# Second mixture normalises and transposes its finished tiles itself; the normalisation stage behind it is dropped

## The chip, the cores and the metric

The kernel runs on one core of a Trainium2 chip, as one program. The metric is the device time of an execution in microseconds (us). Three runs of the kernel before gave 3135.24, 3126.11 and 3123.97, median 3126.11.

## The reference, cut to what matters

Four gated layers run over x, 32 tiles of 128 rows by 128 features (float32); each layer is a cross attention and a mixture, and each adds its output to x. The change lies between the mixture of layer 1 (the second mixture) and the attention of layer 2:

```python
x = x + tanh(g_ffn[1]) * L1_ffn(layernorm(x))          # the mixture
lat = layer_norm(layernorm(x), ln_l_g, ln_l_b)          # input of layer 2's attention
q = lat @ Wq;  k, v = split(concat([ctx_normed, lat], axis=1) @ Wkv)

def L1_ffn(x):      # 8 experts, the two best of each row, and a shared one
    for e in range(8):   # each expert: 64 hidden columns
        y = (silu(x @ gate[e].T) * (x @ up[e].T)) @ down[e].T
        out += where(row chose e, y * mean_weight[e], 0)
    return out + mlp(x, shared weights)                  # 128 hidden columns
```

The attention's own input is thus x normalised twice, scaled by ln_l_g and shifted by ln_l_b. Two normalisations in a row are done as one, with the power -0.5 of var * (1 + eps) + eps * eps.

## The kernel before, in words

x (`k.x`) stays in SBUF, 32 tiles. The program is a sequence of stages; each is a block with one instruction stream for each engine, the engines meet at its end, and nothing of the next stage starts earlier. At the start of a stage SyncE's stream clears the semaphores of the stage before it (`zero_last_stage`, line 93), one instruction each, and only then issues its loads. Inside a stage each engine takes its instructions strictly in the written order and waits on semaphores.

`l1_mixture` (line 1613) is the second mixture. It reads the transposed, normalised input from `k.cols`, and works in 8 groups of four tiles (512 columns, one PSUM bank). For each group it has 5 units: c = 0 to 3 are pairs of experts, c = 4 is the shared one.

- TensorE, `layers` (1673): a gate product and an up product of 128 x 512 for each unit, into two banks used in turn, so unit n waits until `silu_done` and `multiplied` of unit n-2. Behind it, for units 0 to 3 of all groups but the last, `keys.project` (137) computes keys of a later stage. After unit 1 of group g it runs `output(g-1)` (1682), 20 products down to the four tiles, into bank `y_ps[g % 2]`. `output(7)` is the last.
- ScalarE: the silu of each gate product (1713), then, for the units that have one, the copy of the projected keys (151), which waits until the DMA of the slot's last keys has landed.
- GpSimd: for units 0 to 3 the product of the gate with the 0/1 mask of the experts (1659). After unit 3 of each group a product that scales weights of a later stage (1664).
- VectorE: gate times up (1743), and after unit 2 of group g `add(g-1)` (1725): x of group g-1 plus the gated output from PSUM (1728), and four `bn_stats` (1732).
- SyncE: stores the keys (156) and loads masks (1640), in turn. A load waits for the mask product that frees its slot.

Then comes `l2_cross` (3043). It calls `normalise_measured` (433) with twice=True, a stage of its own ("n2a" in the names of tiles): VectorE works means and variances out of the `bn_stats` of all 32 tiles (473 to 482), GpSimd takes the power -0.5, eight tiles at a time (line 571 in the profile), VectorE and ScalarE normalise tiles into staging buffers (496, 544), TensorE transposes four tiles into a bank (513), ScalarE copies the bank to `k.cols` with gain and shift (558). `l2_attention` (1750) follows; its first products read `k.cols` (1895, 1903), and its scores (1868) wait for keys loaded by DMA (1828).

## Time and profile before

| | |
|---|---|
| median of three runs | 3126.11 us (3123.97 to 3135.24) |
| profiled execution, first to last instruction (span) | 3116.6 us |
| busy: TensorE 91%, weight loads 72%, VectorE 65%, ScalarE 58%, GpSimd 46% | of the span |
| second mixture, first gate product to last addition | 956.9 to 1096.5 us |
| stage between mixture and attention | 1096.9 to 1110.7 us |
| first product of the attention | 1110.94 us |

The profile gives the span of one execution, taken by the hardware profiler, and for this execution no time of its own beside the span; the runs are timed from outside, so that their median lies 9.5 us above the span. An engine is busy while one of its instructions runs; waits are listed as idle time, with the instruction that ended them. "PE" is TensorE, "PEld" its weight load, "DVE" VectorE, "ACT" ScalarE, "POOL" GpSimd, "SPq" a DMA issued from SyncE. A float32 matmul is recorded as two. PEclk is the granted TensorE clock as a share of 2.4 GHz.

### The profile page before, as it was taken

The page shows a single profiled execution, that of the slowest core. Times are in us where ns is not written, and L with a number is a line of the kernel's source. Part 1 is how long each engine was busy: PE and PEld are TensorE (multiplying, and loading weights), DVE is VectorE, ACT ScalarE, POOL GpSimd, SP SyncE. Part 2 cuts the span into 40 slices and gives each one's busy share as a digit, 9 for nine tenths or more (in the row PEclk, how much of TensorE's full clock was granted, in tenths as well). Part 3 has the DMA queues.
Part 4 walks back from the last instruction along what each step waited for, and adds up shares of the span by engine and source line. Part 5 has one row for each costly group of instructions (what it writes and reads, how often), then busy time and mean ns, then how long its engine had stood idle before and what let it go on. Part 6 is the DMA issues. An engine that isn't in the chain of part 4 may idle for free. (4 is left out here: it accounts for less than half of the span.)

```text
span 3116.6 us, 70141 instructions
## 1 busy us (share of the span) xinstructions
PE 2851.3 (91%) x21784; PEld 2258.1 (72%) x21784; DVE 2019.9 (65%) x7949; ACT 1821.4 (58%) x5322; POOL 1426.3 (46%) x1719
## 2 busy tenths in 40 slices
PE   7999969977998989999999899999999996597999
PEld 5888854434775678888888777888888774486676
DVE  4554436664653356666666469999999999486433
ACT  5777734443553256666666467887888873353333
POOL 2122217762542334444444247878787876552000
PEclk9999979987998999999999898989999985597999
DMA  3000023433763311111111000000000000001000
GB/s 114 6 5 6 5 68 70 81 81 118 264 224 101 118 49 54 56 54 55 56 54 50 13 14 10 14 14 14 13 13 14 14 14 32 2 19 36 7 10 10
DMA packets 99484, 152.01 MB, mean 49 GB/s; under 512 B 11312, under 2 KB 39488, under 8 KB 98752
## 3 DMA queue, kind: packets, MB, share of 16 engines
q1 hardware_dynamic: 99296, 149.96, 16.0%
q8 instruction: 62, 1.02, 0.1%
q14 instruction: 126, 1.03, 0.1%
HBM read 103.33 MB, written 46.47 MB: 48 GB/s over the span
## 5 line engine op out<-in xcount | busy, mean ns | idle before, releaser
L1845 POOL TENSOR_TENSOR l2a_probs<-l2a_probs,l2a_inv 128x1024 f32<-128x1024 f32 x128 | 242.3, 1893 | 371.7 <-DVE l2a_inv L2011 371.7
L1956 ACT ACTIVATE l2a_probs<-l2a_s_ps,l2a_nm 128x256 f32<-128x256 f32 x512 | 236.1, 472 | 199.4 <-DVE l2a_nm L1987 199.3
L2700 DVE MAX8 l3a_top<-l3a_work 128x8 f32<-128x128 f32 x1536 | 314.6, 279 | 0.0
L2486 PEld LDWEIGHTS l3a_l2o_ps<-net_arena 128*128 128x128 f32 x2016 | 275.3, 222 | 51.2 <-issue 40.3
L2355 POOL TENSOR_SCALAR l3a_above<-l3a_score,l3a_top 128x128 f32<-128x128 f32 x512 | 298.8, 601 | 16.4 <-DVE l3a_work L2702 6.5
L2486 PE MATMUL l3a_l2o_ps<-net_arena 128*128 128x128 f32 x2016 | 283.5, 308 | 15.8 <-ACT net_l1f_gate L2562 15.8
L2702 DVE MATCH_REPLACE8 l3a_work<-l3a_top,l3a_work 128x128 f32<-128x128 f32 x1024 | 269.2, 277 | 0.0
L2474 PE MATMUL l3a_l2h_ps<-net_cols,net_arena 128*128 (+1 forms) x1024 | 251.0, 388 | 12.0 <-ACT net_arena L2593 10.5
L2474 PEld LDWEIGHTS l3a_l2h_ps<-net_cols,net_arena 128*128 128x128 f32 x1024 | 185.0, 191 | 64.8 <-ACT net_arena L2593 23.5
L721 ACT ACTIVATE l0a_probs<-l0a_score_ps,l0a_nm 128x128 f32<-128x128 f32 x512 | 179.6, 381 | 75.1 <-DVE l0a_nm L770 75.1
L2593 ACT ACTIVATE net_arena<-l3a_l2h_ps,net_l2f_b 128x256 f32<-128x256 f32 x512 | 210.0, 492 | 16.6 <-PE l3a_l2h_ps L2474 13.7
L2467 PEld LDWEIGHTS l3a_o_ps<-l3a_v,l3a_pT 128*128 128x128 f32 x1024 | 149.7, 218 | 75.7 <-ACT l3a_pT L2552 66.2
L755 POOL TENSOR_TENSOR l0a_v<-l0a_v,l0a_inv 128x1024 f32<-128x1024 f32 x32 | 60.8, 1901 | 301.2 <-DVE l0a_inv L794 301.2
L2467 PE MATMUL l3a_o_ps<-l3a_v,l3a_pT 128*128 128x9 f32 x1024 | 149.4, 274 | 51.7 <-ACT l3a_pT L2552 51.7
L2360 POOL TENSOR_TENSOR l3a_probs<-l3a_probs,l3a_above 128x512 f32<-128x512 f32 x128 | 162.8, 1272 | 44.1 <-ACT l3a_probs L2571 34.5
L1987 DVE TENSOR_REDUCE l2a_nm<-l2a_s_ps 128x2 f32<-128x512 f32 x256 | 159.0, 683 | 28.4 <-PE l2a_s_ps L1868 28.3
L2571 ACT ACTIVATE l3a_probs<-l3a_score,l3a_nm 128x128 f32<-128x128 f32 x512 | 156.1, 395 | 22.3 <-POOL l3a_nm L2339 22.0
L770 DVE TENSOR_REDUCE l0a_nm<-l0a_score_ps 128x4 f32<-128x512 f32 x128 | 82.2, 684 | 125.5 <-PE l0a_score_ps L681 125.5
L2170 DVE SCALAR_TENSOR_TENSOR net_x<-l3f_o_ps,net_weight,net_x 128x128 f32 (+1 forms) x256 | 72.2, 345 | 139.8 <-PE l3f_o_ps L2087 139.3
L2122 ACT ACTIVATE l3f_hidden<-l3f_h_ps 128x512 f32<-128x512 f32 x128 | 76.3, 597 | 146.0 <-PE l3f_h_ps L2078 146.0
L1919 PE MATMUL l2a_side_ps<-net_ident,l2a_probs 128*128 128x128 f32 x1024 | 153.5, 280 | 1.1 <-POOL l2a_probs L1845 0.7
L2087 PEld LDWEIGHTS l3f_o_ps<-net_arena,l3f_hidden 128*128 128x128 f32 x1024 | 124.2, 192 | 29.7 <-issue 18.2
(527 smaller groups left out, 7184.4 us busy)
## 6 DMA issues: line engine op xcount, KB each, us to landing
kv_ahead<-l1a_kept SPq DMA_DIRECT2D x128, 256.0 KB, 2.6
l0f_code<-code_rows SPq DMA_DIRECT2D x32, 512.0 KB, 10.9
l2a_kT<-kv_ahead SPq DMA_DIRECT2D x64, 256.0 KB, 2.6
l2a_v<-kv_ahead SPq DMA_DIRECT2D x64, 256.0 KB, 2.6
l1a_shift<-neg_top SPq DMA_DIRECT2D x16, 512.0 KB, 4.7
l1f_chosen<-mask_code SPq DMA_DIRECT2D x64, 128.0 KB, 3.1
keys_ahead<-l1f_keys_kept SPq DMA_DIRECT2D x32, 256.0 KB, 3.2
l3a_kT<-keys_ahead SPq DMA_DIRECT2D x32, 256.0 KB, 2.7
```

The source lines that it names most:

```text
L721: act.activation(probs[c % 2][:, h, :], score[g][:, i * P:(i + 1) * P], ACT.Exp, bias=nm[:, h:h + 1], accum_out=sums[c % 2][:, h:h + 1]).t ...
L1845: pool.tensor_tensor(p[:, :, :], p[:, :, :], per_row(inv[c % 2][a][:, :, :].rearrange("p i o -> p (i o)"), KV), ALU.mult).then_inc(scaled, 1)
L1956: act.activation(probs[c % 2][a][:, 2 * i + odd, :], s_ps[a][odd][:, i * KV:(i + 1) * KV], ACT.Exp, bias=nm[c % 2][a][:, i, odd:odd + 1], ...
L1987: dve.tensor_reduce(nm[c % 2][a][:, :, odd:odd + 1].rearrange("p i o -> p (i o)"), s_ps[a][odd][:, :].rearrange("p (i s) -> p i s", i=2), ...
L2355: ins = pool.tensor_scalar(above[:, i, :], score[c % 4][:, h, :], top[c % 2][:, ROUNDS - 1, h, 7:8], None, ALU.is_ge)
L2360: pool.tensor_tensor(probs[c % 2][:, hs, :], probs[c % 2][:, hs, :], above[:, :, :], ALU.mult).then_inc(masked, 1)
L2467: ins = pe.matmul(o_ps[:, h, :], pT[n % 2][:, i, :], v[c % 4][:, h, :], start=True, stop=True)
L2474: ins = pe.matmul(h_ps[i][:, n * WIDE:(n + 1) * WIDE], w1[:, expert(u, x), 2 * i + n, :], k.cols[:, ds(group(q, u) * WIDE, WIDE)], start=T ...
L2486: ins = pe.matmul(output_bank(u, x)[:, at:at + D], hidden[2 * x + n][:, i, j * P:(j + 1) * P], w2[:, expert(u, 2 * x + n), i, :], start=(i ...
L2593: ins = act.activation(hidden[x][:, 2 * i + n, :], h_ps[i][:, n * WIDE:(n + 1) * WIDE], ACT.Gelu, bias=b1[:, e, 2 * i + n:2 * i + n + 1])
L2700: ins = dve.max(t[:, step // 2, h, :], src)
L2702: ins = dve.match_replace(work[:, h, :], t[:, step // 2, h, :], src, LOWEST)
```

## The change

Group g is now normalised and transposed inside the mixture. VectorE's `add` writes its `bn_stats` to a local tile; a new `spread(g)` takes mean and variance with four `bn_aggr` and one `tensor_scalar`; GpSimd's `inverse_std(g)` takes the power -0.5 of four values a row; VectorE's `norm_rows(g)` normalises four tiles; TensorE's `turn(g)` transposes them into the output bank `y_ps[g % 2]`, which is free by then; ScalarE's `take_cols(g)` copies the bank to `k.cols` with gain and shift. `output` waits for that copy in place of the addition. `spread(g-1)` follows unit 3 of group g; `inverse_std(g-1)` follows unit 3's mask, ahead of the weight scaling; `norm_rows(g-2)` follows unit 0, `turn(g-2)` and `take_cols(g-2)` unit 2. Two groups are left for the end. The call of `normalise_measured` goes.

```diff
@@ l1_mixture
+        stats, mean_var, veps, rstd = (s.sb(n, [P, G4, w]) for n, w in (("stats", 6), ("mean_var", 2), ("veps", 1), ("rstd", 1)))
+        normed = s.sb("normed", [P, G4, D])
+        gain, shift = k.l2n_w.norms[:, 2:3], k.l2n_w.norms[:, 3:4]
+        x_measured, moments, veps_ready, rstd_ready, rows_ready, turned, cols_ready = (s.sem(n) for n in (
+            "x_measured", "moments", "veps_ready", "rstd_ready", "rows_ready", "turned", "cols_ready"))
@@ gpsimd
+                def inverse_std(g):
+                    pool.wait_ge(veps_ready, g + 1)
+                    pool.wait_ge(rows_ready, G4 * g)
+                    pool.tensor_tensor(rstd[:, :, 0], veps[:, :, 0], k.neg_half[:, 0:G4], ALU.pow).then_inc(rstd_ready, 1)
...
-                    if g == 0:
+                    if g:
+                        inverse_std(g - 1)
+                    else:
                         pool.wait_ge(scaled, E)
                         wn.wait(pool)
                     pool.tensor_tensor(wn.w2[:, g, :, :], wn.w2[:, g, :, :], per_group(wn.scale_all[:, g, :], 4), ALU.mult
                                        ).then_inc(next_scaled, 1)
                 pool.tensor_tensor(wn.bias8[:, :], wn.bias8[:, :], wn.scale8[:, :], ALU.mult).then_inc(next_scaled, 1)
+                inverse_std(NG - 1)
@@ tensor
-                        pe.wait_ge(y_used, g - 1)
+                        pe.wait_ge(cols_ready, g - 1)
...
+                def turn(g):
+                    pe.wait_ge(rows_ready, G4 * (g + 1))
+                    for j in range(G4):
+                        ins = pe.transpose(y_ps[g % 2][:, j * P:(j + 1) * P], normed[:, j, :], k.ident[:, :])
+                    ins.then_inc(turned, 1)
...
                         layers(g, c)
+                        if c == 2 and g >= 2:
+                            turn(g - 2)
...
+                turn(NG - 2)
                 output(NG - 1)
+                turn(NG - 1)
@@ scalar
+                def take_cols(g):
+                    act.wait_ge(turned, g + 1)
+                    act.activation(k.cols[:, g * BANK:(g + 1) * BANK], y_ps[g % 2][:, :], ACT.Identity, scale=gain, bias=shift
+                                   ).then_inc(cols_ready, 1)
...
+                        if c == 2 and g >= 2:
+                            take_cols(g - 2)
                         if c < PAIRS and g + 1 < NG:
                             keys.take(act, (g + 1) * PAIRS + c)
+                take_cols(NG - 2)
+                take_cols(NG - 1)
@@ vector
-                    for t in range(g * G4, (g + 1) * G4):
-                        dve.bn_stats(k.stats[:, t, :], k.x[:, t, :]).then_inc(k.measured, 1)
+                    for j in range(G4):
+                        dve.bn_stats(stats[:, j, :], k.x[:, g * G4 + j, :]).then_inc(x_measured, 1)
+                def spread(g):
+                    dve.wait_ge(x_measured, G4 * (g + 1))
+                    for j in range(G4):
+                        dve.bn_aggr(mean_var[:, j, :], stats[:, j, :]).then_inc(moments, 1)
+                    dve.wait_ge(moments, G4 * (g + 1))
+                    dve.tensor_scalar(veps[:, :, 0], mean_var[:, :, 1], 1.0 + LN_EPS, LN_EPS * LN_EPS, ALU.mult, ALU.add
+                                      ).then_inc(veps_ready, 1)
+                def norm_rows(g):
+                    dve.wait_ge(rstd_ready, g + 1)
+                    if g:
+                        dve.wait_ge(turned, g)
+                    for j in range(G4):
+                        dve.tensor_scalar(normed[:, j, :], k.x[:, g * G4 + j, :], mean_var[:, j, 0:1], rstd[:, j, :],
+                                          ALU.subtract, ALU.mult).then_inc(rows_ready, 1)
...
                         if c == 2 and g:
                             add(g - 1)
+                        if c == 3 and g:
+                            spread(g - 1)
+                        if c == 0 and g >= 2:
+                            norm_rows(g - 2)
+                norm_rows(NG - 2)
                 add(NG - 1)
+                spread(NG - 1)
+                norm_rows(NG - 1)
@@ l2_cross
-    norms = k.l2n_w.norms
-    normalise_measured(nc, k, "n2a", gains=k.l2n_w, twice=True, gain=norms[:, 2:3], shift=norms[:, 3:4])
     l2_attention(nc, k)
```

## Rows read from the trace of the kernel before

**Rows 1.** Busy time of each engine in three stretches, with granted clock, DMA share, GB/s.
```profile
1050.00:1075.00 25.00, 25.00 (x133) 17.18 (x132) 7.90 (x17) 7.20 (x13) 10.05 (x8) 1.00 0.36 123
1075.00:1096.00 21.00, 18.07 (x100) 12.26 (x98) 6.64 (x14) 3.96 (x7) 6.70 (x6) 1.00 0.16 60
1096.00:1112.00 16.00, 7.17 (x39) 5.42 (x40) 8.97 (x38) 9.14 (x17) 6.53 (x4) 0.77 0.01 2
```
**Rows 2.** Timeline, group 5 into 6: start, duration, instruction, idle time before and its releaser.
```profile
1071.49 0.74 DVE L1728 SCALAR_TENSOR_TENSOR net_x<-l1f_y_ps,net_tg,net_x 128x512 f32<-128x512 f32 x1
1073.49 0.69 DVE L1743 TENSOR_TENSOR l1f_hidden<-l1f_u_ps,l1f_gate 128x512 f32<-128x512 f32 x1 [0.36 <-POOL l1f_gate L1659]
1076.28 0.69 DVE L1743 TENSOR_TENSOR l1f_hidden<-l1f_u_ps,l1f_gate 128x512 f32<-128x512 f32 x1 [2.10 <-ACT l1f_gate L1713]
1076.81 1.27 POOL L1659 TENSOR_TENSOR l1f_gate<-l1f_gate,l1f_chosen 128x512 f32<-128x512 f32 x1 [2.19 <-ACT l1f_gate L1713]
1077.12 1.10 PE L1679 MATMUL l1f_g_ps<-net_cols,net_l1f_gate 128*128 128x512 f32 x2 [0.59 <-DVE l1f_hidden L1743]
```
**Rows 3.** Timeline, the last group and the end of the mixture.
```profile
1078.91 4.63 PE L1689 MATMUL l1f_y_ps<-net_l1f_down,l1f_hidden 128*128 128x128 f32 x40
1086.89 1.27 POOL L1659 TENSOR_TENSOR l1f_gate<-l1f_gate,l1f_chosen 128x512 f32<-128x512 f32 x1 [0.45 <-ACT l1f_gate L1713]
1087.92 0.87 DVE L1732 BATCH_NORM_STATS2 net_logits<-net_x 128x6 f32<-128x128 f32 x4
1088.71 1.35 DVE L1743 TENSOR_TENSOR l1f_hidden<-l1f_u_ps,l1f_gate 128x512 f32<-128x512 f32 x2
1090.12 4.73 PE L1689 MATMUL l1f_y_ps<-net_l1f_down,l1f_hidden 128*128 128x128 f32 x40 [0.79 <-DVE l1f_hidden L1743]
1094.89 0.75 DVE L1728 SCALAR_TENSOR_TENSOR net_x<-l1f_y_ps,net_tg,net_x 128x512 f32<-128x512 f32 x1 [4.83 <-PE l1f_y_ps L1689]
```
**Rows 4.** Timeline of the stage that is dropped, to the attention's first product.
```profile
1096.87 0.22 DVE L473 TENSOR_TENSOR n2a_dif<-net_logits 128x32 f32<-128x32 f32 x1 [0.32 <-PEq L1630]
1098.29 0.18 DVE L482 TENSOR_SCALAR n2a_veps<-n2a_var 128x32 f32<-128x32 f32 x1
1101.26 1.94 PE L513 MATMUL n2a_turned_ps<-net_ident,n2a_stage 128*128 128x128 f32 x8 [6.41 <-DVE n2a_stage L496]
1106.74 0.86 DVE L496 TENSOR_SCALAR n2a_stage<-net_x,n2a_mean,n2a_scale 128x128 f32<-128x128 f32 x3 [0.22 <-PE n2a_turned_ps L513]
1107.09 0.42 PEld L513 LDWEIGHTS n2a_turned_ps<-net_ident,n2a_stage 128*128 128x128 f32 x4 [0.63 <-DVE n2a_stage L496]
1107.97 0.77 ACT L558 ACTIVATE net_cols<-n2a_turned_ps,net_l_norms 128x512 f32<-128x512 f32 x1
1110.97 0.69 PE L1895 MATMUL l2a_side_ps<-net_cols,net_arena 128*128 128x128 f32 x4 [1.12 <-PEq L461]
```
**Rows 5.** Groups of GpSimd's power by width: busy us, mean ns, idle before.
```profile
L1372 POOL TENSOR_TENSOR l1a_rs<-l1a_ss,net_neg_half 128x8 f32<-128x8 f32 x16 | 26.3, 1646 | 64.4 <-DVE l1a_ss L1495 64.4
L2424 POOL TENSOR_TENSOR l3a_rstd<-l3a_spread,net_neg_half 128x2 f32<-128x2 f32 x16 | 11.6, 723 | 1.3
```
**Rows 6.** Stretches around three gaps of TensorE, columns as in rows 1.
```profile
968.00:970.00 2.00, 2.00 (x4) 0.87 (x3) 0.69 (x1) 0.00 (x0) 0.67 (x1) 0.54 0.68 234
971.00:972.00 1.00, 1.00 (x9) 1.00 (x8) 0.00 (x0) 1.00 (x2) 0.00 (x0) 0.72 0.82 238
1098.00:1101.00 3.00, 0.00 (x0) 0.00 (x0) 1.18 (x7) 0.52 (x2) 2.45 (x2) 0.50 0.00 0
1104.00:1105.00 1.00, 1.00 (x7) 0.67 (x6) 0.36 (x3) 0.78 (x3) 1.00 (x1) 0.66 0.00 0
1111.00:1115.00 4.00, 3.48 (x18) 3.21 (x20) 0.69 (x1) 1.10 (x3) 0.00 (x0) 0.57 0.41 133
```
**Rows 7.** Timeline: SyncE's first load of a stage; scores; the first table load behind the mixture.
```profile
1111.47 5.72 SPq L1828 DMA_DIRECT2D l2a_kT<-kv_ahead  x3
1114.66 1.28 ACT L1956 ACT_TABLE_LOAD   x1
```

More of the change, by code:

```diff
@@ L1700, in _ @@
                             output(g - 1)
+                turn(NG - 2)
                 output(NG - 1)
+                turn(NG - 1)
             @block.scalar
             def _(act):
+                k.l2n_w.wait(act)
+                def take_cols(g):
+                    act.wait_ge(turned, g + 1)
+                    act.activation(k.cols[:, g * BANK:(g + 1) * BANK], y_ps[g % 2][:, :], ACT.Identity, scale=gain, bias=shift
+                                   ).then_inc(cols_ready, 1)
                 for i in range(PAIRS):
```

## Prediction

> **What bounds the kernel here.** I read the busy time by stretches first. Inside the mixture TensorE is busy 25.00 of 25 us at full clock, VectorE 7.9, ScalarE 7.2 and GpSimd 10.1 [rows 1]: TensorE's own work sets the pace, a group every 16.7 us (that is what its product list costs too: 5 units of 1.72, 4 key projections of 0.86 and an output of 4.63). What is added to TensorE costs its full length; what is added elsewhere costs only where it makes TensorE wait. From 1096 to 1112 us nothing is bound by work: no engine is busy much over half [rows 1]. That stage is a latency chain of 14.1 us, from 1096.87 to the attention's first product at 1110.97 [rows 4]. In the last group of the mixture TensorE has 18.07 of 21 us [rows 1]: it has no keys to project, and waits on the chain of the other engines, so there additions elsewhere do cost.
>
> The timelines then give the slack: between groups VectorE stands idle for 2.10 us before the shared unit's product, and TensorE already waited 0.59 us for that product [rows 2]. In the last group the output starts at 1090.12 behind a wait of 0.79, and the addition starts when it ends, at 1094.89 [rows 3].
>
> **What goes.** From the last product down (its next event is at 1094.89) to the attention at 1110.97 there are 16.1 us, 2.0 of them addition, statistics and the meeting of the engines, which stay.
>
> **What comes inside the loop, on TensorE.** turn(0) to turn(4) stand in groups 2 to 6, where TensorE sets the pace. Four transposes take 0.42 us of weight loads, pitch 0.105 [rows 4]; 5 x 0.43 = 2.15. Of this the wait of 0.59 at 1077.12 gives back 0.43, because what it waits for (keys landing by DMA, then two silus) was started ahead of the turn. Net +1.7; bounds 0 and 2.6. turn(5) stands in the last group between unit 2 and unit 3; the output behind them still has a wait of 0.79 [rows 3], so I cost it at nothing.
>
> **Inside the loop, elsewhere.**
> - VectorE's spread: four bn_aggr, which the trace doesn't show, and a tensor_scalar of 0.18 [rows 4]. The small operations there take 0.18 to 0.22; four bn_stats take 0.87 [rows 3]. I take 0.17 each, 0.95 with two semaphore gaps; bounds 0.5 and 1.2, and, far off, 0.69 each if it costs like a full product. It fits into the idle 2.10 us before the shared product [rows 2]. Cost 0.
> - GpSimd's power of 4 columns: 2 columns take 0.72, 8 take 1.65 [rows 5], so 1.03 on the line between; these two are the bounds. It waits for spread; queued behind it are the weight scaling (a product of the mask's size, 1.27) and the next group's first mask. Unit 3's product ends at 1074.18, spread at 1075.1, power 1076.2, scaling 1077.5; the mask of unit 0 starts 0.7 late against 1076.81 [rows 2]. Its product, and norm_rows behind that (four rows: 0.86 for three [rows 4], so 1.15), must be done before TensorE's unit 2 at 1083.3, and units 0 and 1 wait for older products. SyncE's next mask load and key store, which wait for that mask, are late by 0.7 too, but ScalarE's key copy that needs them lies under the 4.63 us output [rows 3]. Cost 0.
> - ScalarE's take_cols, 0.77 [rows 4], waits for turn and stands ahead of the key copy and the next silu. TensorE's own key projection (0.86) and the turn move the next gate product back as well; it costs about 0.
> - output(g) waits for cols_ready(g-1), which is there some 9 us earlier.
>
> **The last group and the end, in the clock of before.** Unit 3's product still ends at 1089.4: bn_stats of group 6 end at 1088.79, and its mask, from 1086.89 on for 1.27 [rows 3] and 0.43 late, at 1088.6. Then, one behind another:
> - spread(6) 0.95: 1090.3; GpSimd power 1.03 and a gap: 1091.4; norm_rows(6) 1.15: 1092.55. The shared product (0.7) goes in under the power. TensorE, which is done with unit 4 at 1089.3, can only now start turn(6), at 1092.6.
> - The clock. TensorE idle from 1094.85 was granted 0.50 in 1098 to 1101, and when transposes restarted at 1101.26 it stayed there until 1104.68 (the 0.66 of 1104 to 1105), 3.4 us on; in 968 to 972 it was low for 3.4 us too (0.54, then 0.72) [rows 4, 6]. Here TensorE is idle for 3.3 us. I take 3.4 us at 1.2 GHz from 1092.6: turn(6) 0.43 and output(7) 4.73 [rows 3] become 6.9. Bounds: 5.2 (never low) and 10.3 (low throughout). Output ends at 1099.5, where it ended at 1094.85.
> - add(7) and its bn_stats, 1.7: 1101.2. spread(7) 0.95, power 1.1, norm_rows 1.15: 1104.4. turn(7) at the low clock: 8 transposes took 1.94 [rows 4], so 0.95: 1105.35. take_cols 0.8: 1106.15. Engines meet, 0.25: 1106.4.
> Before, that point was 1110.97. The end gives 4.6 us.
>
> **The attention's head.** Its first products start at low clock (before, 0.57 over 1111 to 1115 [rows 6]), now from the first on: +0.3. SyncE clears the semaphores of the stage before: 10 of the dropped stage, done within 0.5 us (first load 1111.47 against first product 1110.97 [rows 4, 7]); now the mixture's 26, 0.8 us more. The keys landed 2.7 us behind their issue, about 0.5 before the first scores; +0.5 with the shift. Head: +0.8, bounds 0 and 1.5.
>
> **Sum.** -4.6 + 1.7 + 0.8 = -2.1 us on the profiled span of 3116.6. I apply it to the median of the runs, 9.5 above the span: 3126.1 - 2.1 = 3124.0 us, 0.07% faster. Best corner: spread 0.5 (twice on the path, -0.9), power 0.72 (-0.6), no low clock (-1.7), head 0 (-0.8), turns in waits (-0.5): -6.6. Worst: spread 1.2 and power 1.65 (+0.5, +1.2), low throughout (+3.4), head (+0.7), turns (+0.9): +4.6.
>
> One rule of the Trainium skill speaks against this step. "TensorE: Matmul & The Clock Gate" (Part 4: PE-mode transpose) says that transposes do not count as busy work, so that full clock doesn't engage on them. The rows don't agree: between 1094.85 and 1104.68 TensorE did nothing but transposes, and the clock rose while it did them [rows 4, 6]. By the rule turn(6) would not help the clock back, and output(7) would run its first 3.4 us at half, 0.4 more: a sum of -1.7 in place of -2.1.
>
> **Rivals.**
> 1. The cover in the loop doesn't hold (slower). If bn_aggr costs like a full product, 0.69, spread is 3.0 and outlasts VectorE's 2.10 of idle time; the shared product comes late, and TensorE's unit 1 of the next group, already at its limit (0.59 wait [rows 2]), waits. It decides from a spread of about 2.5 on (2.10 and the turn's 0.43). Price: 0.5 x 6 groups, and 2.05 more twice in the end: +7.1, so +5.0: 3131. For it: no row shows bn_aggr, and the shared product waits in order behind it. Against: every small operation in the stage takes about 0.2.
> 2. The silu's table is reloaded behind each Identity. A load takes 1.28 [rows 7]. Six in the loop: +7.7, 3132 in all. Against: the dropped stage ran Identity behind the last silu, and the first load after it is the exponential's at 1114.66 [rows 7]; for it, no row shows a silu behind an Identity. The Trainium skill's "ScalarE: Activation LUTs" (Table sets: the hidden batching unit) has identity in every set, by which this rival is worth 0.
> 3. The end is shorter than I price: the clock holds through the gap and the small operations are cheap; -6, 3120. For it: 0.50 for the whole of a stretch shows first from 1098 on [rows 6], 3.1 us into the idle time, and this gap has 3.3.
> 4. The stage's whole 14 us are won, its chain hidden under the products: 3112. Against: only six of eight groups are hidden; the last two stand one behind another behind the last masks.
>
> **Chances.** Forecast 0.64, rival 1 0.12, rival 2 0.03, rival 3 0.17, rival 4 0.01, something I don't see 0.03. The single time is 3124.0. The three runs before differ by 11 us, so the median moves by a few us by itself; range 3117 to 3132, which leaves out rival 4 and the far ends. A measurement of this kernel tells about 0.5% (15.6 us) from no change; every case but the fourth's extreme and the unseen ones lies within: faster 0.02, same 0.95, slower 0.03.
>
> **What would show it.** After: turn in the loop 0.42 us for four, groups 17.1 us apart instead of 16.7; bn_aggr near 0.17; the power near 1.0; the last output starting some 3 us later behind a wait of TensorE on norm_rows, with the granted clock at 0.50 in it; about 7 us from its end to the attention's first product instead of 16.1; the first key load 1.3 us behind the stage's start. It is wrong if TensorE shows new waits inside groups 2 to 6, if a table load shows behind take_cols, or if the output starts at its old time.

## The result, and the profile of the changed kernel

| | before | after |
|---|---|---|
| median of the runs | 3128.61 us (3123.97 to 3135.24, 4 runs) | 3108.74 us (3103.28 to 3112.15, 4 runs) |
| span of the profiled execution | 3116.6 us | 3106.5 us (its run: 3108.43) |

The ratio of after to before is 0.9936, 95% interval 0.9916 to 0.9955: 0.64% faster, 15 us below the forecast of 3124.0 and outside its range (3117 to 3132). The medians differ by 19.9 us and the spans by 10.1. Wherever both are known, an execution's time is only 1.7 to 2.7 us above its own span, so most of the 9.5 us between span and median of the kernel before is not the way of timing, as I had put it: its profiled execution was a quick one.

**The mixture, as changed.** Busy time by stretches of the kernel after (TensorE, weight loads, VectorE, ScalarE, GpSimd, then clock, DMA share and GB/s, as in [rows 1]):

```profile
1050.00:1075.00 25.00, 25.00 (x149) 18.45 (x148) 9.35 (x23) 8.95 (x15) 8.59 (x7) 1.00 0.36 121
1075.00:1096.00 21.00, 17.02 (x78) 10.02 (x76) 11.75 (x35) 5.00 (x9) 11.19 (x10) 0.96 0.25 87
1096.00:1112.00 16.00, 10.05 (x55) 9.49 (x56) 3.45 (x15) 1.80 (x3) 1.01 (x1) 0.71 0.01 2
```

TensorE is still busy for all of the first stretch: the new work of the other engines is covered there, VectorE's 9.35 us against 7.90 before. The timeline of the kernel after, group 5 into 6 and the last group:

```profile
1057.26 0.74 DVE L1759 SCALAR_TENSOR_TENSOR net_x<-l1f_y_ps,net_tg,net_x 128x512 f32<-128x512 f32 x1
...
1072.26 0.60 PE L1707 MATMUL l1f_y_ps<-net_ident,l1f_normed 128*128 128x128 f32 x4
1072.90 0.78 ACT L1730 ACTIVATE net_cols<-l1f_y_ps,net_l_norms 128x512 f32<-128x512 f32 x1 [0.70 <-PE l1f_y_ps L1707]
1074.31 0.74 DVE L1759 SCALAR_TENSOR_TENSOR net_x<-l1f_y_ps,net_tg,net_x 128x512 f32<-128x512 f32 x1
1074.65 0.60 ACT L1740 ACTIVATE l1f_gate<-l1f_g_ps 128x512 f32<-128x512 f32 x1 [0.26 <-PE l1f_g_ps L1691]
1077.37 0.37 DVE L1768 BATCH_NORM_AGGREGATE l1f_mean_var<-l1f_stats 128x2 f32<-128x6 f32 x4
1078.03 1.01 POOL L1662 TENSOR_TENSOR l1f_rstd<-l1f_veps,net_neg_half 128x4 f32<-128x4 f32 x1 [1.36 <-DVE l1f_veps L1770]
...
1093.90 1.26 POOL L1675 TENSOR_TENSOR net_arena<-net_arena 128x512 f32<-128x512 f32 x1
1093.96 2.20 DVE L1778 TENSOR_SCALAR l1f_normed<-net_x,l1f_mean_var,l1f_rstd 128x128 f32<-128x128 f32 x4 [0.52 <-POOL l1f_rstd L1662]
1096.22 1.11 PE L1707 MATMUL l1f_y_ps<-net_ident,l1f_normed 128*128 128x128 f32 x4 [3.92 <-DVE l1f_normed L1778]
1097.12 6.56 PE L1701 MATMUL l1f_y_ps<-net_l1f_down,l1f_hidden 128*128 128x128 f32 x40
1103.72 0.75 DVE L1759 SCALAR_TENSOR_TENSOR net_x<-l1f_y_ps,net_tg,net_x 128x512 f32<-128x512 f32 x1 [7.56 <-PE l1f_y_ps L1701]
1107.12 1.11 DVE L1778 TENSOR_SCALAR l1f_normed<-net_x,l1f_mean_var,l1f_rstd 128x128 f32<-128x128 f32 x4 [1.12 <-POOL l1f_rstd L1662]
1108.29 1.11 PE L1707 MATMUL l1f_y_ps<-net_ident,l1f_normed 128*128 128x128 f32 x4 [4.61 <-DVE l1f_normed L1778]
1110.53 1.20 PE L1949 MATMUL l2a_side_ps<-net_cols,net_arena 128*128 128x128 f32 x4 [1.12 <-PEq L1635]
1111.90 0.82 SPq L1882 DMA_DIRECT2D l2a_kT<-kv_ahead  x2
```

A group is 17.05 us long (the addition at 1057.26 and again at 1074.31), against 16.63 before. The last output product starts at 1097.12 where it stood at 1090.12 [rows 3], but only 6.85 us lie between its end and the attention's first product at 1110.53, where 16.1 us lay before. The additions of groups 1 and 6, with the five turns of the loop between them, lie 84.03 us apart after and 82.59 before, 1.44 more. Counted from the mixture's first gate product (956.93 before, 956.84 after), the attention starts at +154.04 before and +153.69 after. So the whole edit has earned 0.35 us in these two profiles, and nearly all of the 10.1 us of the span are elsewhere.

**Where they are.** The same first product of layer 3's attention starts at 1755.87 before and 1755.73 after; GpSimd's last comparison of scores in that stage comes 10.0 us earlier (2662.2 and 2652.2), and from there to the end the distance stays at 10. The diff doesn't touch this stage. The ScalarE, TensorE and SyncE streams of this stage are loops of some 102 us a pass, whose end is a branch back to their start; VectorE's and GpSimd's are unrolled. VectorE sets its pace. VectorE is busy for 93.83 of 100 us before and 99.86 after. Of the kernel before: busy time in 2050 to 2150; what VectorE (1950 to 2560) and ScalarE (2000 to 2560) waited for, as engine, line, what it waited for: us in total, times, longest; and three rows of the timeline:

```profile
2050.00:2150.00 100.00, 96.37 (x577) 81.69 (x577) 93.83 (x598) 76.82 (x198) 76.34 (x126) 0.86 0.05 14
```
```profile
DVE l3a_inv L2709 <- PE l3a_o_ps L2467: 9.5, 5, 3.1
ACT L2571 <- issue: 8.7, 5, 1.9
```
```profile
2025.70 1.08 ACT L2583 ACTIVATE l3a_score<-l3a_s_ps 128x512 f32<-128x512 f32 x2 [2.20 <-PE l3a_s_ps L2450]
2028.58 1.28 ACT L2571 ACT_TABLE_LOAD   x1 [1.79 <-issue]
2079.13 0.26 DVE L2709 RECIPROCAL l3a_inv<-l3a_o_ps 128x16 f32<-128x16 f32 x1 [3.15 <-PE l3a_o_ps L2467]
```

and of the kernel after, where ScalarE has no line with "issue":

```profile
2050.00:2150.00 100.00, 96.70 (x624) 83.78 (x620) 99.86 (x639) 83.68 (x212) 83.38 (x136) 0.93 0.05 14
```
```profile
DVE l3a_inv L2763 <- PE l3a_o_ps L2521: 0.9, 1, 0.9
```
```profile
2025.75 1.09 ACT L2637 ACTIVATE l3a_score<-l3a_s_ps 128x512 f32<-128x512 f32 x2 [2.20 <-PE l3a_s_ps L2504]
2026.86 1.28 ACT L2625 ACT_TABLE_LOAD   x1
2075.88 0.26 DVE L2763 RECIPROCAL l3a_inv<-l3a_o_ps 128x16 f32<-128x16 f32 x1
```

The two traces run level to 2026.8. There ScalarE's loop branches back. Before, nothing goes on for 1.79 us that the profile could put down to another engine ("issue"); after, it goes on at once. It happens behind each of the five branches back, 8.7 us in all. Later in the pass VectorE finds TensorE's product 3.15 us late, and the waits of that kind sum to 9.5 us before and 0.9 after. Pass by pass (from the branch records) ScalarE's loop takes 109.6, 102.3, 102.4, 102.5 and 105.6 us before, and 102.37 five times after. The page's line on code fetches (queue: packets, MB), before and after, names the suspect:

```profile
q14 instruction: 126, 1.03, 0.1%
```
```profile
q14 instruction: 101, 0.83, 0.1%
```

These are packets of 8 KB, 25 more before, and they lie in these passes: 12, 12, 11, 13, 11 a pass before, 7, 8, 6, 7, 6 after. After, that is what the unrolled engines alone need: 670 records of VectorE and 202 of GpSimd in the first pass, at 64 bytes an instruction, make 55.8 KB, or 6.8 packets. The five more of a pass before are enough for ScalarE's 367 instructions (23.5 KB). The trace doesn't say for which engine a packet is; that they are ScalarE's is inferred, and e1 below bears it out.

Ahead of that loop ScalarE's trace has 16 records fewer after: 8 activations (the dropped stage had 16, the mixture has 8 more), 7 semaphore instructions and a drain at a stage's end. So the loop begins 16 places, 1024 bytes, earlier. The compiled ScalarE program is 22 entries shorter, the number that I used when I planned the runs. But it holds 169 placeholders before and 163 after that leave no record. Without them the programs of ScalarE, VectorE, GpSimd and SyncE have 12,994 instructions after, 0.83 MB, which is what queue 14 fetched (TensorE's 16,073 make the 1.03 MB of queue 8): the placeholders are not in the fetched code, and 16 is the shift. The places of loops below are counted so.

### The profile page after: what moved, and what is told of

Its sections match the earlier page's. It is cut to its first block and busy times, and to the rows that moved or that the text cites. A ratio compares the mean times of both kernels' runs of the same rounds, so it can differ in the third digit from the quotient of the medians.

```text
span 3106.5 us, 70161 instructions
## 1 busy us (share of the span) xinstructions
PE 2845.7 (92%) x21784; PEld 2260.2 (73%) x21784; DVE 2029.1 (65%) x7986; ACT 1824.0 (59%) x5314; POOL 1430.8 (46%) x1723
## 3 DMA queue, kind: packets, MB, share of 16 engines
q1 hardware_dynamic: 99296, 149.96, 16.1%
q8 instruction: 63, 1.03, 0.1%
## 5 line engine op out<-in xcount | busy, mean ns | idle before, releaser
L2754 DVE MAX8 l3a_top<-l3a_work 128x8 f32<-128x128 f32 x1536 | 327.4, 347 | 0.0
L2756 DVE MATCH_REPLACE8 l3a_work<-l3a_top,l3a_work 128x128 f32<-128x128 f32 x1024 | 277.6, 346 | 0.0
L2528 PE MATMUL l3a_l2h_ps<-net_cols,net_arena 128*128 (+1 forms) x1024 | 251.1, 388 | 11.2 <-ACT net_arena L2647 9.2
L2756 DVE MATCH_VALUE_LOAD l3a_work<-l3a_top,l3a_work 128x8 f32 x1024 | 150.3, 150 | 0.0
```

The costliest lines, as they stand in the source:

```text
L2528: ins = pe.matmul(h_ps[i][:, n * WIDE:(n + 1) * WIDE], w1[:, expert(u, x), 2 * i + n, :], k.cols[:, ds(group(q, u) * WIDE, WIDE)], start=T ...
L2754: ins = dve.max(t[:, step // 2, h, :], src)
L2756: ins = dve.match_replace(work[:, h, :], t[:, step // 2, h, :], src, LOWEST)
```

## Experiments

Added waits are on semaphores long set; two fit in an instruction. "Gap" is the longest time without an instruction of ScalarE's that follows the loop's branch, from the trace's records: 1.42 to 1.71 us before, one instruction behind the branch, and 0.19 to 0.21 after. The view's 8.7 us of "issue" are five such gaps and some 0.17 us more each.

**e1, e2, e3: the place given back.** The kernel after with 16 more instructions on ScalarE, 10 on TensorE, or both:

```
def padded(eng, k, name, n):
    if name == "n2f":
        for _ in range(n):
            k.gates_fetch.wait(eng)
+               padded(act, k, name, 32)     # e1 and e3
+               padded(pe, k, name, 20)      # e2 and e3
```


> The changed kernel with 16 more instructions on ScalarE (waits on a long finished DMA, two to an instruction) at the start of the stage ahead of layer 3's attention, where ScalarE is idle. ScalarE's code behind it then lies where it lay in the kernel before. Theory A: the time was won in layer 3's attention, because ScalarE's loop there lies at another place and fetches its code sooner behind the branch (1.62 us ahead of the second instruction before, 0.20 after): the loop's periods go back from 102.4 us to up to 108, and the span grows by about 10 us. Theory B: TensorE's code position does it, not ScalarE's: no change (within 2 us). Theory C: nothing of position, the difference lies between executions: no change of the mean, and periods that differ from run to run in both kernels.

> The changed kernel with 10 more instructions on TensorE's queue at the same place, ScalarE's code where it is after the change. Theory A: no change, ScalarE's gap behind its branch stays at 0.20 us and the periods at 102.4. Theory B: about 10 us longer. Theory C: no change.

> The changed kernel with both, 16 on ScalarE and 10 on TensorE: both queues' code at the places of before. Theory A: like 16 on ScalarE alone, some 10 us above the changed kernel. Theory B: like 10 on TensorE alone, some 10 us. If only this one is slow, the two together are needed. Theory C: no change.

**e4: the change left out, the place taken.** The kernel before, where VectorE takes over the eight tiles that ScalarE normalised in the stage of the change:

```
-        by_act = (0, 3) if gain is None else (3,)
+        by_act = (0, 3) if gain is None else ()
... (TensorE's wait for ScalarE's tiles and norm_some are left out where by_act is empty)
```


> The kernel before, whose dropped stage is kept, but VectorE normalises all its tiles and ScalarE none: ScalarE has 14 instructions fewer ahead of layer 3's attention (the change takes 16), TensorE 3 fewer. The stage itself should be longer by up to 2 us. Theory A: layer 3's attention gets the 102.4 us periods of the changed kernel, and the whole is some 8 us faster than the kernel before, with none of the change in it. Theories B and C: as the kernel before, or 2 us slower.

| | median (range), runs | ratio to before (95%) | gap | packets a pass |
|---|---|---|---|---|
| e1 ScalarE +16 | 3123.61 (3105.97 to 3135.58), 10 | 0.9975 (0.9948 to 1.0003) | 1.42 to 1.49 | 11 to 13 |
| e2 TensorE +10 | 3106.87 (3103.26 to 3113.49), 5 | 0.9918 (0.9891 to 0.9945) | 0.19 to 0.21 | 6 to 8 |
| e3 both | 3119.15 (3102.11 to 3137.48), 10 | 0.9974 (0.9948 to 1.0) | 1.43 to 1.69 | 11 to 13 |
| e4 before, ScalarE -14 | 3105.67 (3100.52 to 3115.79), 7 | 0.993 (0.9905 to 0.9954) | 0.19 to 0.21 | 6 to 7 |

The kernel before on this chip: 3129.49 (3114.92 to 3147.53, 23 runs). The whole change with the gap (e1, e3) is no longer told from the kernel before; the kernel before without the gap (e4) has all of the gain. On one chip the gap costs 12 to 17 us in the median (e3 and e1 against e2). TensorE's place does nothing. One thing went against the expectation: e1's profiled execution has the gap and yet five passes of 102.4 us and a span of 3105.9. The gap does not lengthen a pass each time; it takes away slack, and some executions then lose 3 or 7 us in a pass and others none. A single pass of 105.5 to 106.0 us also stands in six profiles without the gap (e2, e6, e7, e11, e12, e13), so the loss of 3 us is made likelier by it and not brought by it alone; passes of 109 us stand only with it. In sets of five runs or more the times spread over 19 to 35 us with the gap and 7 to 15 without.

**e5: the kernel before, loop further back.** If places repeat with the packets' 8 KB, a loop 128 instructions behind its place in after has no gap. I took the loop of the kernel before to lie 22 behind that place, and added 106:

```
                 if gain is not None:
-                    gains.wait(act)
+                    for _ in range(213):
+                        gains.wait(act)
```


> The kernel before with 106 instructions MORE on ScalarE (waits on a weight load that is long complete, in front of the norm stage behind the mixture, where ScalarE idles while the last output product runs). With the 22 instructions that ScalarE's program had less in the kernel after, this puts the layer-3 loop 128 instructions of 64 bytes, that is 8 KB, behind its place in the kernel after. Theory A (what counts is where the loop lies against steps of 8 KB, the size of the code packets in the trace): gap behind the branch about 0.20 us, 6 to 8 packets of 8 KB in a pass, passes of 102.3 to 102.4 us, median 3105 to 3111 us although nothing of the change is in it. Rival 1 (fewer instructions ahead of the loop is what helped): gap 1.6 us, 12 packets, median 3127 us or more. Rival 2 (the change itself brought the 20 us): median 3126 to 3131 whatever the gap.

Measured: 3149.09 (3135.03 to 3157.36, 6 runs) against 3121.0 for before (3110.26 to 3128.96, 11 runs), ratio 1.0105 (1.0085 to 1.0125). The loop of the kernel before lies 16 behind and not 22, so here it lay at +122 and not at +128, and this run doesn't speak against theory A in this form. In e5's trace (ScalarE's waits, the same columns)

```profile
ACT L2572 <- issue: 19.1, 5, 3.9
```

two gaps stand behind each branch, of 1.4 to 1.7 and, one instruction on, 2.0 to 2.3 us, with 11 to 13 packets a pass, as with one gap. (Some 5.4 us of its loss are the padding itself, which held up ScalarE's tiles in the dropped stage: 21.5 us from the last addition to the attention where before has 16.1.)

**e9 to e12: a scan of the place**, the kernel after with 8, 64, 128 or 256 more instructions in ScalarE's router stage:

```
                 act.activation(p[:, :, :], p[:, :, :], ACT.Sigmoid).then_inc(squashed, 1)
+                for _ in range(16):        # 128, 256; e12: 256 here, 256 in the mixture
+                    k.l1r_w.wait(act)
```


> The kernel after with 8 instructions more on ScalarE (waits on a load long complete, in the router stage, where ScalarE idles), so that its layer-3 loop starts 8 instructions (512 bytes) later; good at 0 and +2 so far, bad at +16 and +22, worse at +128. Theory A (place of the loop alone): a gap of either 0.20 or 1.4 to 1.7 us behind each of the loop's branches, nothing between, with 6 to 8 or 11 to 13 packets a pass; it narrows the edge to between +2 and +8, or +8 and +16. Rival (each instruction more costs its share): a gap between, about 0.9 us.

> The same with 64 instructions (4 KB). Theory A with places that repeat every 8 KB is already refuted by +128 of the kernel before; if they repeat every 4 KB this has a gap of 0.20 us. If there is one edge and all beyond it is bad (the loop, some 367 instructions, no longer fits with what the fetch holds), it has 1.4 us or more in one or two places. If the count of code packets that a pass must fetch decides, gap and packets (11 to 13) go together here too.

> The same with 128 instructions (8 KB): ScalarE's loop lies where it lay in the kernel before with 106 more, all else is of the kernel after. Theory A (place of ScalarE's loop alone): two gaps in each pass, 1.6 and 2.0 us, passes of 105 us or more, the span 15 us or more longer than that of after (3106.5). Rival (the stream of another engine in the kernel before, TensorE's or SyncE's, made the second gap): one gap or none, passes of 102.4 us.

> The same with 256 instructions (16 KB), 128 of them at the end of the mixture (up to 6 us of waiting there that belong to the padding). If places repeat every 16 KB the gap is 0.20 us and a pass 102.3 to 102.4 us, with 6 to 8 packets; if only beyond 16 KB or never, gaps of 1.4 us or more stay.

One execution each: +8 3105.28, +64 3127.21, +128 3113.24, +256 3109.46. The gap is 0.2 us at +8, +128 and +256, and about 1.5 at +64, whose view of waits reads

```profile
ACT L2627 <- issue: 8.6, 5, 1.9
DVE l3a_inv L2765 <- PE l3a_o_ps L2523: 21.5, 10, 3.0
```

with passes of 109.3, 102.5, 105.4, 109.3 and 109.2 us. There is no value in between, so it isn't the number of instructions. e11's expectation took +128 for e5's place; by the records it is six further on.

**e13 to e16: the kernel before with a good place, an edge, and the other engines' programs.**

```
                 # e13: kernel before, e14: kernel after, in the router stage as above
+                for _ in range(236):       # e14: 250
+                    k.l1r_w.wait(act)
+                padded(pool, k, name, 32)  # e15 (e16: dve), kernel after
```


> The kernel before with 118 instructions more on ScalarE (waits on a load long complete, in the router stage, where ScalarE idles), nothing of the change. The loop of layer 3's attention on ScalarE has 367 instructions (branch to branch); three pieces of 128 instructions (8 KB) have 384, so only 17 of 128 places let it lie within three pieces. Theory B (it must lie within three pieces; the place is counted from a base that differs by a few instructions between the two kernels): shifts of after by 0, +8, +128, +256 are within, +16 and +64 are not; the kernel before with 106 more (two gaps) lies one place ahead of the window, so 118 more lies 12 places further, within it: gap 0.20 us behind the branch, 6 to 8 packets, passes of 102.3 us but for single ones of 105.6, median 3105 to 3112 us, 10 to 20 below the kernel before. Rival 1 (the kernel before has the gap for a reason in another engine's program or data, whatever ScalarE's place; then the 14 instructions fewer of an earlier run were luck): gap of 1.4 us or more, median 3120 to 3150. Rival 2 (the place does not cost the time, the change does): gap 0.20 but median 3120 or more.

> The kernel after with 125 instructions more on ScalarE in the router stage, 3 fewer than the 128 that had no gap. Theory B with the window's first place at -2 (what follows if the base of the kernel before lies 3 lower, by which GpSimd's program is shorter): the loop's first instruction or two lie in a fourth piece, so two gaps in a pass, 1.6 and 2.0 us, passes of 105 us or more. If the window's first place lies at -3 to -8: gap 0.20 as with +128. If each place has its own luck: anything.

> The kernel after with 16 instructions more on GpSimd (long true waits at the start of layer 2's last norm stage), none on ScalarE. If ScalarE's place is counted from a base that moves with GpSimd's program, this is the same as 16 more on ScalarE: gap 1.4 us behind the branch, 11 to 13 packets. Rival (base independent of GpSimd's program): gap 0.20 us, 6 to 8 packets.

> The same with 16 instructions more on VectorE. If the base moves with VectorE's program: gap 1.4 us. Rival (it does not; VectorE's program differs by 36 instructions between the two kernels, which would put 22 more in the kernel before at a place that it does not behave like): gap 0.20 us, 6 to 8 packets.

e13: 3109.3 (3100.59 to 3113.67, 10 runs) against 3127.16 for before (3113.21 to 3137.54, 15 runs), ratio 0.994 (0.9922 to 0.9959), gap 0.19, 6 to 8 packets a pass. Nothing of the change is in it, 118 instructions are added that compute nothing, and it gains what the change gains. This shows the cause without the change. e14 (3106.75, gap 0.19) refutes the edge that I had put just above its place; e15 (3110.52) and e16 (3112.36), gap 0.20 both, say that GpSimd's and VectorE's programs don't move the place.

Counted by records from the loop's place in after, the places without a gap are 0, +2 (e4), +8 (e9), +125 (e14), +128 (e11), +134 (e13) and +256 (e12). Those with one are +16 (before, e1, e3) and +64 (e10), and +122 (e5) has two. The two kernels need no separate rule: the good places can be one stretch that begins at +123 and repeats, and ends between +8 and +16.

**e6, e7, e8: the last group.** e6 keeps GpSimd's weight scaling from running beside the normalising of group 6; e7 puts the last output product first; e8 is both:

```
+                    if g == NG - 1:                      # e6, e8
+                        pool.wait_ge(rows_ready, G4 * g)
                     pool.tensor_tensor(wn.w2[:, g, :, :], ...
-                turn(NG - 2)                             # e7, e8
                 output(NG - 1)
+                turn(NG - 2)
                 turn(NG - 1)
```


> The kernel after with one wait more on GpSimd: its last product with the next weights (last group) waits for the four normalised tiles of group 6. If the 2.20 us of those four beside GpSimd's product are contention between VectorE and GpSimd, they take 1.10 to 1.15 us now, as the four of group 7 do where GpSimd is idle (1.11), the transposes of group 6 and the last output product start 1.05 us earlier, and the end of the mixture comes 1.0 to 1.3 us earlier against its first gate product. Rival (the first group of a stretch of four is slow by itself, whatever GpSimd does): 2.1 to 2.3 us still and no shift. In either case ScalarE's layer-3 loop keeps its place: gap 0.20 us.

> The kernel after with two calls of TensorE exchanged at the end: the last output product (group 7) goes ahead of the transposes of group 6, into the other bank. If the chain of the path (shared product of group 7, inverse root and rows of group 6, their transposes, output product) is what made the output product late, it now starts at about +136 us from the first gate product (after: +140.3, before: +133.2), ends at full clock about 5.0 us later (after: 6.56 us long), and attention's first product comes 4.5 to 6 us earlier than in the kernel after: median 3102 to 3105 us. Rival 1 (the transposes of group 6 and the evacuation that follow on the output product are late next, since ScalarE and TensorE have them both in a row at the end): gain of only 2 to 3 us, median 3106. Rival 2 (layer 2's attention waits for something else, its first key load, in any case): no gain, 3108 to 3109.

> Both of the last two edits together. If the contention's 1.1 us is off the path once the output product goes first, the time is that of the exchanged calls alone within 0.3 us (3102 to 3105). If the rows of group 6 still hold back VectorE's last residual sum, it is 1 us lower.

**e17, e18: after and e7 again**, on one chip.

> The kernel after, unchanged, for its spread and as the yardstick of the next run on the same chip. Theory: median 3104 to 3110 us, 0.5 to 0.7% below the kernel before; ScalarE's loop in layer 3 with a gap of 0.20 us and 6 to 8 packets a pass, as in its first profile. Rival (its place in memory is drawn anew each time it is loaded): gap or packets differ from the first profile.

> The kernel after with the last output product ahead of the transposes of group 6, against the kernel after on the same chip. Its attention starts 6.85 us earlier against the first gate product in the one profile, and 4.7 us earlier than in the profiles where the low clock falls as it does in most of the variants (151.5). Theory: 4 to 7 us below the kernel after (ratio to it about 0.998). Rival (given back by the clock later): within 2 us of the kernel after.

| | median (range), runs | ratio to before (95%) | last output starts, ends | attention starts |
|---|---|---|---|---|
| after, first profile | 3108.74 | 0.9936 (0.9916 to 0.9955) | +140.29, +146.84 | +153.69 |
| e17 after | 3108.65 (3103.41 to 3110.72), 6 | 0.9924 (0.9902 to 0.9947) | +139.24, +144.78 | +151.63 |
| e6 | 3105.21, 1 | | +138.67, +144.45 | +151.29 |
| e7 | 3100.32 (3097.28 to 3106.07), 6 | 0.9944 (0.9925 to 0.9963) | +135.26, +140.00 | +146.84 |
| e8 | 3103.46 (3101.63 to 3108.64), 6 | 0.9952 (0.9934 to 0.9971) | +135.69, +140.43 | +147.26 |
| e18 as e7 | 3100.14 (3098.14 to 3108.05), 6 | 0.9902 (0.9879 to 0.9925) | +136.69, +141.42 | +148.27 |

Each ratio is to the kernel before on its own chip and hour: 3121.0 beside e6 to e8, 3130.07 beside e17 and e18. The last columns are us from the mixture's first gate product. Other runs with the mixture of after have the attention at +151.35 to +151.65 (e1, e3, e11, e12, e14, e15, e16), +153.57 (e2), +153.69 (e10) and +148.75 (e9); e13, with the mixture and the stage of before, has +154.91. e17 kept its gap of 0.20 on a new load. The row of e6's timeline that answers to the 2.20 above:

```profile
1093.39 1.11 DVE L1780 TENSOR_SCALAR l1f_normed<-net_x,l1f_mean_var,l1f_rstd 128x128 f32<-128x128 f32 x4 [0.52 <-POOL l1f_rstd L1662]
```

With GpSimd's product out of the way the four tiles take 1.11 us, not 2.20: the contention is shown. But the output product starts only 0.6 us and the attention 0.3 us earlier than in e17, not 1.05; with the last output first it gains nothing (e8 against e7). The exchange is worth more: TensorE's last products of e7,

```profile
1087.93 4.73 PE L1701 MATMUL l1f_y_ps<-net_l1f_down,l1f_hidden 128*128 128x128 f32 x40 [1.21 <-DVE l1f_hidden L1790]
1092.49 0.60 PE L1707 MATMUL l1f_y_ps<-net_ident,l1f_normed 128*128 128x128 f32 x4
1097.26 1.12 PE L1707 MATMUL l1f_y_ps<-net_ident,l1f_normed 128*128 128x128 f32 x4 [4.17 <-DVE l1f_normed L1778]
1099.50 0.76 PE L1949 MATMUL l2a_side_ps<-net_cols,net_arena 128*128 128x128 f32 x2 [1.12 <-PEq L1635]
```

show the output at full clock (4.73 for 6.56) straight behind the shared product, and group 6's transposes in its shadow. The attention starts 4.8 us earlier than in e17 (5.4 with e18 against the first profile, where the early low-clock period lies alike). On one chip e18's median is 8.5 us below e17's (3100.14 and 3108.65) and its mean 6.0; their ranges overlap and so do the intervals of their ratios to before. Against before on its own chip e7 (0.9944) is no better than after (0.9936 and 0.9924), so that the gain in time rests on e17 and e18, while the earlier start of the attention stands in both profiles. This order of the calls has the lowest medians here.

## Why the prediction was wrong

**The step that failed** is the sum: "-4.6 + 1.7 + 0.8 = -2.1 us on the profiled span", applied to the median. It holds only if no stage outside these three changes, and I never wrote this down as a step, let alone gave it bounds; it stood in the 0.03 of "something I don't see".

What the runs put in its place: the edit takes 16 instructions out of ScalarE's program ahead of the loop of layer 3's attention. The loop gets to a place where the gap behind its branch is 0.2 instead of 1.4 to 1.7 us, and VectorE, which sets the pace there, waits less. That stage is 10.0 us shorter in the two profiles, and in the medians the gap costs 12 to 17 us (e3 and e1 against e2). e4 and e13 have that gain without the change; e13 is 17.9 us below the kernel before on its chip.

Rival 4's 3112 lies nearest to the measured 3108.7, by luck: it was to win the dropped stage's whole 14 us, and the attention starts only 0.35 us (first profile) and 2.41 us (e17) earlier.

The row was there to be read: the 8.7 us of "issue" waits on one engine inside a loop, on the line of waits of ScalarE, in the kernel before. I looked only at the stretches that the diff touches.

The Trainium skill names a mechanism that would do this. "Runtime: NRT & Kernel Launch" (Instruction fetch mechanics) says that most engines hold 32 KiB of instructions, two pages of 16 KiB, and that a taken branch to a target outside the two must fetch that page first. By that rule a loop of 367 instructions (23.5 KB) is free of fetches if it lies in two pages, which 146 of 256 places allow. The runs agree: a stretch of 146 good places from +123 on that repeats every 256 holds +125, +128, +134 and +256, and 0, +2 and +8 with them, and leaves out +16, +64 and +122. e5's two gaps with one instruction between them are what a loop would have that begins on the last place of a page. But the packets of queue 14 are of 8 KB, and a stretch of 18 good places from +123 on that repeats every 128 (three pieces of 8 KB hold 384 instructions) fits all these runs too. A place such as +192, which would tell them apart, was not run. That the pieces are pages held by the engine, and which size they have, is therefore argued and not shown; that the place of the loop makes the gap is shown.

**The steps, one by one.**
- Turns in the loop, +0.43 a group: right (17.05 against 16.63; the wait of 0.59 gave back 0.32 and not 0.43; net 1.44 against 1.7), as is the cover: spread took 0.37 + 0.17 in place of 0.95, the power 1.01 (1.03), take_cols 0.78, and no new wait of TensorE shows in 1050 to 1075.
- Rivals 1 and 2 are dead by the same rows: bn_aggr is below 0.15 us, and a silu (1074.65) follows on an Identity (1072.90) with no table load.
- turn(6) was to start at 1092.6 and 1.7 later for the turns, 137.4 us from the first gate product: it did so at 139.4, in e17 at 138.3. The term that was mis-sized: norm_rows(6), 1.15 from rows of a stage in which no GpSimd product ran beside it, took 2.20 beside GpSimd's weight scaling. The other 1.0 us of the first profile is clock. Before and in e17 a low-clock period of 3.4 us began 11.2 to 11.4 us from the first gate product, in a stretch where TensorE was held up anyway; in the first profile of after it came at 18.0. Rows by stretch of after; before, 968 to 970 had 0.54 [rows 6]:

```profile
968.00:971.00 3.00, 3.00 (x15) 1.80 (x14) 0.69 (x1) 0.20 (x1) 0.55 (x1) 1.00 0.72 205
975.00:978.00 3.00, 3.00 (x7) 1.52 (x6) 0.81 (x2) 0.60 (x1) 1.26 (x1) 0.50 0.40 154
```

- Low clock once TensorE has idled: right in kind. turn(6) and output(7) took 7.46 us (1096.22 to 1103.68), 6.4 in e17; forecast 6.9. From turn(6)'s start the clock stayed at 0.50 for 4.9 us, in e17 for 2.8; forecast 3.4. Rival 3, that the clock holds, is wrong.
- From the output's end to the attention: 6.85, forecast 6.9.
- Head: forecast +0.8, measured +0.5 (first product to first scores 3.78 before, 4.27 after). The first key load is issued 1.37 behind the first product where it was 0.5, as forecast (1.3), but this costs nothing: in both kernels the scores wait for ScalarE's copy of keys. The 0.5 are the low clock, under which the first four products take 0.99 in place of 0.52 us to the next. Before, then after:

```profile
1111.49 1.89 PE L1903 MATMUL l2a_side_ps<-net_cols,net_arena 128*128 128x128 f32 x8
1114.75 2.06 PE L1868 MATMUL l2a_s_ps<-l2a_kT,l2a_qT 64*128 64x256 f32 x16 [0.52 <-ACT l2a_kT L1964]
```
```profile
1111.52 1.92 PE L1957 MATMUL l2a_side_ps<-net_cols,net_arena 128*128 128x128 f32 x8
1114.80 2.00 PE L1922 MATMUL l2a_s_ps<-l2a_kT,l2a_qT 64*128 64x256 f32 x16 [0.52 <-ACT l2a_kT L2018]
```

- Local sum at the attention's first product: forecast -2.9 (the -2.1 without the head's 0.8), measured -0.35 in the first profile, -2.41 in e17. The mechanism of the edit was right, and its size within 0.5 us where the clock lies alike; but it is 2 us in a result of 20.
- The best corner of the range takes 0.5 us off for the turns, where their own lower bound of 0 would take off 1.7: -7.8 and not -6.6. Neither reaches the result.

## What to carry to other kernels

A change of code moves every loop behind it, on each engine: before pricing an edit, look for waits on "issue" behind loop branches in all stages, and count them as at stake with either sign. If a kernel gets faster or slower in a stage that the diff doesn't touch, compare the code packets and these waits first, count the engine's records ahead of the loop in both traces, and give the old kernel the new placement with idle instructions before crediting the change. And put what is late (the last output) ahead of what is only next in order (the transposes of the group before).

## What the runs showed that I had not expected

- A loop of 367 ScalarE instructions has, by its place alone, a gap of 0.2 us behind the branch back or one of 1.4 to 1.7 us with some 5 packets of 8 KB more a pass; at one place (e5) two gaps, 3.7 us together. Over five passes the view shows 8.7 us of waits, and the stage is up to 23 us longer (no longer in e1's profile, 10.0 in that of before, 23.2 in e10's, against after).
- Four f32 tensor_scalar of 128x128 with one tensor input take 1.11 us on VectorE, and 2.20 beside a GpSimd product of 128x512.
- Whether a late engine costs anything differs from pass to pass and from execution to execution: with the same gap, passes of 102.4, 105.6 and 109.3 us stand side by side.
- The compiled program is not the fetched one: each engine's has 169 (before) or 163 (after) placeholders that the trace and the code packets don't show, and six of them were enough to send a run (e5) to the wrong place.
